# Layer 0 of a graph network: neighbour sums as one split matmul a tile, with the rest subtracted on GpSimd

## The reference, cut to what matters

```python
h = jnp.maximum(_layernorm(x, axis=-1), 0.0)
deg = jax.ops.segment_sum(jnp.ones_like(src, jnp.float32), dst, num_segments=n)
inv_deg = jnp.where(deg > 0, 1.0 / jnp.maximum(deg, 1.0), 0.0)[:, None]

def sage(h, w_self, w_neigh, b):
    agg = jax.ops.segment_sum(h[src], dst, num_segments=n) * inv_deg
    return h @ w_self + agg @ w_neigh + b
h = jax.nn.relu(sage(h, ws0, wn0, b0))      # 128 -> 256
h = jax.nn.relu(sage(h, ws1, wn1, b1))      # 256 -> 256
out = x + sage(h, ws2, wn2, b2)             # 256 -> 128
```

## Time and profile before

| | |
|---|---|
| median of 3 runs | 3842.36 us (3839.69 to 3842.39) |
| profiled execution | 3837.3 us |
| its span, first to last instruction | 3835.5 us |
| busy: TensorE | 3503.3 us (91%) |
| busy: VectorE | 3342.0 us (87%) |
| busy: ScalarE | 3085.1 us (80%) |
| busy: GpSimd | 2557.9 us (67%) |
| mean granted TensorE clock | 0.923 of full speed |

### The profile page before, as it was taken

How to read it: one execution, slowest core, us unless ns; L and a number is a source line. 1 busy time by engine, 2 the same in 40 slices (tenths; PEclk the granted TensorE clock), 3 DMA queues, 4 the chain that set the end, 5 groups by cost and what they waited for, 6 DMA issues and landing times. The chain is left out here.

```text
span 3835.5 us, 100978 instructions
## 1 busy us (share of the span) xinstructions
PE 3503.3 (91%) x22513; PEld 3162.4 (82%) x22513; DVE 3342.0 (87%) x9695; ACT 3085.1 (80%) x8036; POOL 2557.9 (67%) x3691
## 2 busy tenths in 40 slices
PE   1999999999999999999998999999999986777777
PEld 1888888888888888888887999998999976666666
DVE  7999999999999999999986888988988977777777
ACT  4888888888888888888886877878887867777777
POOL 2666666666666666666555777777777767777776
PEclk9999999999999999999999999999999986566555
DMA  2444444444444444444444888888888879999998
GB/s 75 138 143 143 144 142 144 143 144 144 144 143 144 143 142 143 142 143 144 141 145 143 247 245 247 249 248 244 247 246 246 249 216 263 262 262 266 262 265 249
DMA packets 828104, 727.99 MB, mean 190 GB/s; under 512 B 90198, under 2 KB 699614, under 8 KB 827918
## 3 DMA queue, kind: packets, MB, share of 16 engines
q1 hardware_dynamic: 642069, 570.14, 45.9%
q0 software_dynamic: 80336, 104.91, 11.5%
q10 hardware_dynamic: 105600, 51.92, 4.5%
HBM read 451.32 MB, written 361.23 MB: 212 GB/s over the span
## 5 line engine op out<-in xcount | busy, mean ns | idle before, releaser
L1445 PE MATMUL ps_out<-w_hi,hid_hi 128*128 128x512 f32 (+1 forms) x3136 | 1142.3, 364 | 27.3 <-DVE layer_mem L1336 24.7
L610 POOL DMA_INDIRECT loaded_rows<-in_x,gather_at x784 | 904.0, 1153 | 390.2 <-issue 241.7
L1445 PE MATMUL ps_out<-w_hi,hid_lo 128*128 128x512 f32 (+1 forms) x3136 | 1054.6, 336 | 0.0
L1445 PE MATMUL ps_out<-w_lo,hid_hi 128*128 128x512 f32 (+1 forms) x3136 | 1049.7, 335 | 0.0
L646 POOL DMA_INDIRECT layer_mem<-pq_rows,gather_at x784 | 788.2, 1005 | 273.2 <-issue 215.7
L1445 PEld LDWEIGHTS ps_out<-w_hi,hid_hi 128*128 128x128 f32 x3136 | 589.3, 188 | 135.4 <-issue 51.6
L659 POOL DMA_INDIRECT layer_mem<-zy_rows,gather_at x528 | 526.0, 996 | 182.3 <-issue 141.3
L1445 PEld LDWEIGHTS ps_out<-w_hi,hid_lo 128*128 128x128 f32 x3136 | 588.8, 188 | 68.8
L1445 PEld LDWEIGHTS ps_out<-w_lo,hid_hi 128*128 128x128 f32 x3136 | 591.1, 188 | 55.1
L750 ACT ACTIVATE layer_mem<-ps_hid,b_col 128x256 f32<-128x256 f32 x784 | 329.1, 470 | 211.4 <-PE ps_hid L1445 193.7
L837 ACT ACTIVATE layer_mem<-iota_row,triple_node 128x128 f32<-128x128 f32 x1056 | 337.3, 390 | 154.3 <-DVE layer_mem L1378 57.5
(11 more groups left out here) (172 smaller groups left out, 8817.2 us busy)
## 6 DMA issues: line engine op xcount, KB each, us to landing
pq_rows<-layer_mem SPq DMA_DIRECT2D x392, 512.0 KB, 3.2
loaded_rows<-pq_rows SPq DMA_DIRECT2D x392, 256.0 KB
zy_rows<-layer_mem SPq DMA_DIRECT2D x392, 256.0 KB
loaded_rows<-zy_rows SPq DMA_DIRECT2D x264, 192.0 KB, 4.1
layer_mem<-in_x SPq DMA_DIRECT2D x264, 192.0 KB
out_rows<-layer_mem ACTq DMA_DIRECT2D x264, 192.0 KB
loaded_rows<-in_x SPq DMA_DIRECT2D x392, 128.0 KB, 2.2
loaded_rows<-in_x,gather_at POOLq DMA_INDIRECT x784, 2.9
```

The source lines that it names most:

```text
L610: pool.indirect_dma_start(raw[s.slot][0:rows, 2 + j, :], None, table, bass.IndirectOffsetOnAxis(gather_at[s.slot][0:rows, j:j + 1], axis=0 ...
L1445: ins = nc.tensor.matmul(o, a, b, start=n == 0, stop=n == len(terms) - 1)
```

## The change

In layer 0 the neighbours are split as well. ScalarE rounds `h_nbr` (with its ones) into the first half of a new tile `halves`, GpSimd subtracts that from `h_nbr` and writes the rest beside it, and TensorE multiplies `select`, now as float32r, by both at once: 260 columns a tile, in one PSUM bank a tile. VectorE adds the sums of the rests in one more instruction. `ps_agg` grows to two banks, and `ps_hid` shrinks to one buffer. GpSimd's subtraction stands behind the gathers in its step, for the pair three steps back. ScalarE normalises the neighbours ahead of the own rows. Layer 1's `nbr_hi` and `nbr_lo` become views of `halves`.

```diff
-        nbr_hi = [sb(f"nbr_hi{i}", [P, L1_SPLIT, H], FP32R) for i in range(2)]
-        nbr_lo = [sb(f"nbr_lo{i}", [P, L1_SPLIT, H], FP32R) for i in range(2)]
+        halves = [sb(f"halves{i}", [P, 2, 2, D + 2], FP32R) for i in range(2)]
+        nbr_hi, nbr_lo = ([t[:, :, :, :].rearrange("p j t f -> p (j t f)")[:, at:at + H].rearrange("p (j f) -> p j f", j=1)
+                           for t in halves] for at in (0, H))
...
-        ps_agg, ps_turn = (ctx.enter_context(nc.psum_tensor(f"ps_{k}", [P, 512], FP32)) for k in ("agg", "turn"))
-        ps_hid = [ctx.enter_context(nc.psum_tensor(f"ps_hid{i}", [P, 512], FP32)) for i in range(2)]
+        ps_agg = ctx.enter_context(nc.psum_tensor("ps_agg", [P, 1024], FP32))
+        ps_turn, ps_hid = (ctx.enter_context(nc.psum_tensor(f"ps_{k}", [P, 512], FP32)) for k in ("turn", "hid"))
...
+        agg_bank = [ps_agg[:, j * 512:j * 512 + 2 * (D + 2)] for j in range(2)]
+        hi_sums, lo_sums = (ps_agg[:, :].rearrange("p (j f) -> p j f", j=2)[:, :, at:at + D + 2] for at in (0, D + 2))
...
@@ GpSimd, behind the gathers @@
                     t, u = first.back(2), first.back(3)
+                    if u.live():
+                        pool.wait_ge(L0.nbr_hi_ready, u.n + 1)
+                        if u.has(2):
+                            pool.wait_ge(L0.summed, u.back(2).n + 1)
+                        pool.tensor_tensor(halves[u.half][:, :, 1, :], h_nbr[u.half][:, :, :],
+                                           halves[u.half][:, :, 0, :].bitcast(FP32), ALU.subtract
+                                           ).then_inc(L0.nbr_split, 1)
...
@@ ScalarE @@
-                        act.wait_ge(L0.own_added, t.n + 1)
+                        act.wait_ge(L0.rest_added, t.n + 1)
...
                         if t.has(2):
-                            act.wait_ge(L0.summed, t.back(2).n + 1)
+                            act.wait_ge(L0.nbr_split, t.back(2).n + 1)
                             act.wait_ge(L0.turned, t.back(2).n + 1)
-                        for j in range(4):
-                            rows = h_own[t.half][:, j, :] if j < 2 else h_nbr[t.half][:, j - 2, 0:D]
+                        for j in range(2, 4):
+                            rows = h_nbr[t.half][:, j - 2, 0:D]
...
+                        last.then_inc(L0.nbr_normed, 1)
+                        for j in range(2):
+                            last = act.activation(h_own[t.half][:, j, :], raw[t.slot][:, j, :], ACT.Relu,
+                                                  bias=shift[t.half][:, j:j + 1], scale=rstd[t.half][:, j:j + 1])
                         last.then_inc(L0.normed, 1)
+                        act.wait_ge(L0.nbr_normed, t.n + 1)
+                        if t.has(2):
+                            act.wait_ge(L0.summed, t.back(2).n + 1)
+                        act.activation(halves[t.half][:, :, 0, :], h_nbr[t.half][:, :, :], ACT.Copy
+                                       ).then_inc(L0.nbr_hi_ready, 1)
...
@@ VectorE; L1229 and L1231 read hi_sums in place of rows @@
                     dve.reciprocal(inv_degree[:, two], degree[s.half][:, :]).then_inc(L0.recip_done, 1)
+                    dve.wait_ge(L0.own_added, s.n + 1)
+                    dve.tensor_tensor(agg[s.half][:, :, 0:D], agg[s.half][:, :, 0:D], lo_sums[:, :, 0:D], ALU.add
+                                      ).then_inc(L0.rest_added, 1)
...
@@ TensorE @@
-                    if t.has(2):
-                        pe.wait_ge(L0.h1_made, t.back(2).n + 1)
+                    if t.has(1):
+                        pe.wait_ge(L0.h1_made, t.back(1).n + 1)
...
-                    pe.wait_ge(L0.normed, t.n + 1)
+                    pe.wait_ge(L0.nbr_split, t.n + 1)
                     if t.has(1):
                         pe.wait_ge(L0.degree_done, t.back(1).n + 1)
-                        pe.wait_ge(L0.own_added, t.back(1).n + 1)
+                        pe.wait_ge(L0.rest_added, t.back(1).n + 1)
...
-                        last = nc.tensor.matmul(ps_agg[:, j * H:j * H + D + 2], select[t.half][:, j, :].bitcast(FP32),
-                                                h_nbr[t.half][:, j, :], start=True, stop=True)
+                        last = nc.tensor.matmul(agg_bank[j], select[t.half][:, j, :],
+                                                halves[t.half][:, j, :, :].rearrange("p t f -> p (t f)"),
+                                                start=True, stop=True)
```

More of the change, by code:

```diff
@@ L298, in build @@
         b2_held = ps_out[1][:, 0:D]
-        strips = [ps_agg[:, D + 2 + j * H:D + 2 + j * H + TP] for j in range(2)]
+        strips = [ps_agg[:, j * 512 + 2 * (D + 2):j * 512 + 2 * (D + 2) + TP] for j in range(2)]
         w_loaded, bias_loaded = sem("w_loaded"), sem("bias_loaded")
@@ L749, in step @@
                         for m in range(2):
-                            last = act.activation(h1[t.half][:, m, :], ps_hid[t.half][:, m * PAIR:(m + 1) * PAIR],
+                            last = act.activation(h1[t.half][:, m, :], ps_hid[:, m * PAIR:(m + 1) * PAIR],
                                                   ACT.Relu, bias=b0_col[:, m:m + 1])
@@ L771, in step @@
                         if t.has(2):
[L772 removed]
+                            act.wait_ge(L0.nbr_split, t.back(2).n + 1)
                             act.wait_ge(L0.turned, t.back(2).n + 1)
[L774 to L776 removed]
+                        for j in range(2, 4):
+                            rows = h_nbr[t.half][:, j - 2, 0:D]
+                            if general:
                                 last = act.activation(rows, raw[t.slot][:, j, :], ACT.Copy)
@@ L1080, in general @@
                         dve.wait_ge(ge_turned, i + (first + 1))
-                        mine(dve.tensor_scalar(ge_same[:, :], ps_hid[1][0:EP, 0:EP], ge_dst[:, :], None,
+                        mine(dve.tensor_scalar(ge_same[:, :], ps_hid[0:EP, 0:EP], ge_dst[:, :], None,
                                                op0=ALU.is_equal))
@@ L1106, in general @@
                         dve.wait_ge(ge_summed, i + (first + 1))
-                        dve.tensor_tensor(ge_new[:, 0:width], ps_hid[0][0:EP, 0:width], ge_cur[:, 0:width],
+                        dve.tensor_tensor(ge_new[:, 0:width], ps_turn[0:EP, 0:width], ge_cur[:, 0:width],
                                           ALU.add).then_inc(ge_new_ready, 1)
@@ L1225, in layer0 @@
                     two = bass.ds(s.n * 2, 2)
-                    rows = ps_agg[:, :].rearrange("p (j f) -> p j f", j=2)
                     if with_sums:
                         with_sums()
-                    dve.scalar_tensor_tensor(degree[s.half][:, :], rows[:, :, D], fast[:, :], base_degree[:, two],
+                    dve.scalar_tensor_tensor(degree[s.half][:, :], hi_sums[:, :, D], fast[:, :], base_degree[:, two],
                                              op0=ALU.mult, op1=ALU.add).then_inc(L0.degree_done, 1)
                     dve.scalar_tensor_tensor(agg[s.half][:, :, 0:D], h_own[s.half][:, :, :], fast[:, :],
-                                             rows[:, :, 0:D], op0=ALU.mult, op1=ALU.add).then_inc(L0.own_added, 1)
+                                             hi_sums[:, :, 0:D], op0=ALU.mult, op1=ALU.add).then_inc(L0.own_added, 1)
                     dve.wait_ge(L0.degree_done, s.n + 1)
                     dve.reciprocal(inv_degree[:, two], degree[s.half][:, :]).then_inc(L0.recip_done, 1)
+                    dve.wait_ge(L0.own_added, s.n + 1)
+                    dve.tensor_tensor(agg[s.half][:, :, 0:D], agg[s.half][:, :, 0:D], lo_sums[:, :, 0:D], ALU.add
+                                      ).then_inc(L0.rest_added, 1)
                 if t.live():
@@ L1424, in general @@
                         pe.wait_ge(ge_spread, i + (first + 1))
-                        nc.tensor.matmul(ps_hid[1][0:EP, 0:EP], ge_dst_b[:, :], ident[0:EP, 0:EP],
+                        nc.tensor.matmul(ps_hid[0:EP, 0:EP], ge_dst_b[:, :], ident[0:EP, 0:EP],
                                          is_transpose=True, start=True, stop=True).then_inc(ge_turned, 1)
@@ L1430, in general @@
                             pe.wait_ge(ge_msg_ready, i + 1)
-                        nc.tensor.matmul(ps_hid[0][0:EP, 0:width], ge_same[:, :], ge_msg[:, 0:width],
+                        nc.tensor.matmul(ps_turn[0:EP, 0:width], ge_same[:, :], ge_msg[:, 0:width],
                                          start=True, stop=True).then_inc(ge_summed, 1)
@@ L1452, in layer0 @@
                     pe.wait_ge(L0.lo_ready, t.n + 1)
-                    if t.has(2):
-                        pe.wait_ge(L0.h1_made, t.back(2).n + 1)
+                    if t.has(1):
+                        pe.wait_ge(L0.h1_made, t.back(1).n + 1)
                     for m in range(2):
                         out_features = slice(m * P, (m + 1) * P)
-                        last = product(ps_hid[t.half][:, m * PAIR:(m + 1) * PAIR],
+                        last = product(ps_hid[:, m * PAIR:(m + 1) * PAIR],
```

10 lines of the change are left out of this document (5 added, 5 removed).

## The result

The changed kernel takes 4332.55 us, median of 4 runs (4324.93 to 4341.94), against 3842.38 us before: a ratio of 1.128 with a 95% interval of 1.126 to 1.130, 490 us slower. The prediction said 4230 us, 4060 to 4420. In a second set of runs it took 4324.71 against 3839.47 us, 485 us more, where I had expected 480 to 500.

A forecast was written before the change was run, and what follows sets the result against it. TensorE was taken to bound layer 0 at 5.05 us a pair; a new loop through GpSimd, its terms summing to 6.04, adds 388 us over 392 pairs to 3837.3, plus 5 for the median: 4230 us, range 4060 to 4420.

The forecast's parts named there:

- the loop: Layer 0: one pair's sums wait, through GpSimd's gathers and subtraction, on the previous pair's sums; 6.04 us a pair, chance 0.75.
- The subtraction with its stall: Loop term on GpSimd: 0.76 us for the 128x260 subtraction plus 0.20 us of stall on VectorE.
- Sums to `degree`: Loop term from the start of TensorE's neighbour sums to `degree` on VectorE: 0.54 us.
- The gathers' part: Loop term on GpSimd from `self_scale` to the end of the second gather: 3.57 us, ends 3.28 and 3.81.
- The hand-over to TensorE: Loop term from the subtraction's end to the start of TensorE's sums: 0.06 us.
- each spread: Low and high ends for subtraction, gathers and stall: loop of 5.22 us (3910 us) to 6.67 us (4477 us).
- TensorE's saving: Layer 0 sums as two 260-column matmuls, not four of 130: 0.21 us a pair saved, hidden under the longer loop.
- VectorE becomes the bound: Rival: VectorE's work plus waits sets layer 0's pace at 5.19 to 5.28 us a pair, 3895 to 3935 us; chance 0.07.
- ScalarE's loop: Rival: sums, transposes, normalisation, rounding, subtraction, next sums take 4.91 us, pace about 5.05; chance counted inside the VectorE case.
- The clock: Rival: TensorE, idle part of the time in layer 0, drops to a lower clock; 4370 to 5600 us, chance 0.05.
- The idle time ahead of the sums: Sign: TensorE idles about 1.2 us a pair before the sums, over 400 us in all, ended by GpSimd's write of `halves`.
- The two matmuls: Sign: TensorE's sums appear as two matmuls of 128x260 about 0.12 us apart.

The follow-up runs named there:

- e1: Changed kernel with GpSimd making `self_scale` one step later, for the pair four steps back: 4542.59 us, +265 us against the kernel before on the same chip.
- e2: Changed kernel with the subtraction issued between the two gathers of a step instead of behind both: 4447.19 us, +170 us against the kernel before on that chip.
- e9: Kernel before plus a like GpSimd subtraction behind the gathers, into a tile nobody reads, so TensorE doesn't wait for it: 3890.31 us, ratio 1.013.
- e8: Changed kernel with `self_scale` one step later and the subtraction between the two gathers: 3958.88 us, ratio 1.031 against the kernel before.
- e5: Changed kernel without GpSimd's subtraction (rests zero) and without VectorE's add of the rests' sums: 4250.26 us, ratio 0.993 against the kernel before on that chip.
- e6: Kernel before with one edit, `ps_hid` as a single buffer: 4276.71 us, ratio 0.9999 against the kernel before on the same chip.
- e3: Changed kernel with the subtraction cut to four numbers a partition, the other rests zero: 4577.58 us, +300 us against the kernel before on that chip.
- e7: Changed kernel with the subtraction on VectorE, first in its step, instead of GpSimd: 4486.87 us, +208 us against the kernel before on that chip.

## Why the prediction was right

**Where it goes.** Right, and shown: the loop sums, `degree`, `self_scale`, gathers, subtraction, sums can be read off the timeline, and cutting it at either of two places (e1, e2) gives back 220 and 315 of 485 us, while a like instruction outside of it (e9) costs 51. That is the prediction's own mechanism, and not only its number.

**Its length.** 6.04 us predicted, 6.27 on average over 48 pairs, 6.29 over the stretch; added time 388 us predicted, 490 measured. Four terms were off. The subtraction with its stall was 0.86 and not 0.96: alone it takes 0.70, below the 0.76 that I took, and stalls add 0.16. Sums to `degree` was 0.11 longer: in 24 of the 48 pairs VectorE stands idle and `degree` still starts 0.61 or 0.62 us after the sums, for which I have no cause, and in some others VectorE is late for it (0.79 behind the addition of `b_rows`). The gathers' part was 0.13 longer. The hand-over to TensorE is 0.10 at least, and 0.17 on average. Of the 12 late ones, four follow the end of `select`, which is the VectorE instruction that the subtraction holds up (26.1 us of 1000 in the row of L1494 above go to `select`); in the other eight `select` had long ended, and the cause is open. So the collision was priced on GpSimd's side and left out on VectorE's, but inside this loop the part left out is small. It shows in e1, e2 and e8, where `hid_lo` and `select` lengthen VectorE's work.

That the commonest pair takes the very 6.04 us of the sum is luck. In it `degree` is 0.08 later, the gathers' part 0.14 longer and the hand-over 0.04 longer than predicted, and the subtraction, undisturbed, 0.26 shorter. The range's text also says that it takes in about half of each spread. At the lower end it does; 4420 us is 6.52 us a pair, three quarters of the way from 6.04 to 6.67, and half would have been 4354. The measured 4332.55 lies below that too.

**TensorE's saving.** Right in size (0.21 predicted, 0.18 to 0.20 seen in e5) and right that it is worth nothing while another loop decides. The product for `ps_hid` eats 0.05 of it: most of its matmuls follow each other at 0.120 us in the changed kernel and at 0.113 in the kernel before. The runs say what it isn't. e6 has the single `ps_hid` and not the slower matmuls, e9 has them with two `ps_hid` and unsplit sums, and e5 without any subtraction. What e9, e5 and the changed kernel share against the kernel before and e6 is larger tiles declared ahead of `cat_hi` and `cat_lo` (`apart` in e9; `halves` takes 64 bytes a partition more than `nbr_hi` and `nbr_lo` together), so the place of the operands in SBUF is a candidate; no run tests it.

**VectorE.** The add lasts 421 ns against the 470 I took from L1231. The rival "VectorE becomes the bound" was right as the next bound: e8 ends there.

**ScalarE's loop.** It never decided; ScalarE waited 196.6 us of 1000 ahead of `cat_hi` in the changed kernel.

**The clock.** It stayed at 0.99 to 1.00 in layer 0 with TensorE busy 81% and idle for about 1 us a pair, so that rival is out.

**Signs.** The idle time ahead of the sums came out as forecast (180.9 us over 159 pairs, 1.14 a pair), but the profile gives most of it to "issue" and only 43 us of 1000 to `halves`. The two matmuls start 0.20 us apart and not 0.12, which they do only where TensorE hasn't waited (e5). Whoever reads the waits alone doesn't find the subtraction; the timeline shows its end 0.10 us before the start of the sums in most pairs.

**The rule on shared ports.** By the Trainium skill's SBUF — State Buffer, Who interferes with whom, a VectorE instruction with two SBUF inputs contends with a GpSimd one that reads SBUF, and one with at most one SBUF input doesn't, unless it runs in a mode that uses both pairs of ports, which a copy can enter. The runs agree. In e1 `select` lasts 0.905 us (median of 106) where it overlaps the subtraction and 0.416 elsewhere. The addition of `b_rows`, which reads PSUM and SBUF, keeps its 0.68 us in 19 overlaps in e1, and the statistics, with one SBUF input, keep their 0.42 in 211 overlaps in e8. (`cat_lo` says nothing here: in e1 it never runs beside the subtraction.) The copy of eight keys in the key search has one SBUF input and is held all the same, here in e2 until the subtraction ends; alone it takes 0.17 us:

```profile
1103.73 0.70 POOL L624 TENSOR_TENSOR halves<-h_nbr,halves 128x260 fp32r<-128x260 f32 x1
...
1103.84 0.62 DVE L1023 COPY keys<-best_now 88x8 f32 x1 [0.18 <-DVE best_now L1018]
```

## What to carry to other kernels

Busy shares say which engine is full; they don't say what a new wait closes. Before an instruction is put behind others on an engine, write down what those others wait for, and follow the chain until it comes back to the same engine: if it returns within one step, its whole length, gathers and all, is the new pace. Such a loop is often cut by moving a cheap instruction whose result isn't due for several steps, not by making the new one faster. And when two engines hold each other up, price the stall on both sides: it is as long as the other's instruction, not as one's own. An experiment that adds an instruction can also move what it doesn't mean to move: compare the engine that binds, instruction by instruction, before the whole difference is put down to the one added.

## What the runs showed of the hardware

- A GpSimd subtraction of 128x260 float32 takes 0.69 to 0.70 us undisturbed (median 700 ns over 392, up to 1643). With 128x4 it takes 0.21. That is 1.9 ns a column. With one tile as both operands (e9) 128x260 has a median of 0.63 us.
- It is held while VectorE runs an instruction with two SBUF operands, even when it has four numbers a partition to do (1.05 us in e3), and it holds such instructions in turn (`select` 0.42 to 1.07 us in e1) and a copy of eight numbers (0.17 to 0.62 us in e2).
- A gather of 128 rows keeps GpSimd 1.00 to 1.05 us when neither `hid_lo` nor `select` runs in its first 0.35 us, and 1.37 us (median of 148, kernel before) when one does.
- TensorE's matmuls of 128x256 in float32r followed each other at 0.113 us in some kernels and at 0.120 in others (before and e6 against e9, e5 and the changed kernel), at a granted clock of 0.99 to 1.00. The cause is open.
- A VectorE subtraction of the same 128x260 took 423 ns (e7).
- Two chips ran layer 0 at the same pace (5.05 us a pair before, 5.06 in e6) and differed by 438 us in the whole, with 194 against some 247 GB/s moved in layer 1. Everything outside layer 0 took 1862 to 1869 us on the one and 2291 to 2297 on the other.
